# The join of a graph layer and two attentions: row sums added early, graph sums added from PSUM, three projected rows ahead

## The reference, cut to what matters

```python
xn = _layernorm(x)
x2 = x + _L0_gnn_ref(xn, edge_index, ...) + _L0_mix_ref(xn[None], ...)[0]
out = x2 + _L0_ffn_ref(_layernorm(x2)[None], ...)[0]
# _L0_gnn_ref: two relational layers; a layer sums over each node's incoming edges
# _L0_mix_ref: kernel attention of 12 heads; its end, with x meaning xn:
y = xn + heads @ W_proj + b_proj
return (y - mu) * rsqrt(var + LN_EPS) * gamma + beta
# _L0_ffn_ref: softmax attention of 12 heads on the normalised x2, with a router
# (x2n @ Wg.T) and low-rank parts (x2n @ A) that need "logits" of 136 columns per row
```

## Time and profile before

| what | us |
|---|---|
| median of 3 runs (lowest, highest) | 2971.27 (2967.63, 2975.25) |
| the profiled execution, its own time | 2969.1 |
| its span, first to last instruction | 2967.3 |
| mean granted TensorE clock, share of 2.4 GHz | 0.955 |

### The profile page before, as it was taken

One profiled execution on the slowest core, in us unless ns is written; L12 is line 12 of the kernel. 1 busy time (PEld: TensorE's weight loads), 2 busy tenths in 40 slices (PEclk: granted clock), 3 DMA queues, 4 the chain that ended last, 5 costly groups with the idle time before them and its releaser, 6 DMA issues.

```text
span 2967.3 us, 65252 instructions
## 1 busy us (share of the span) xinstructions
PE 2651.6 (89%) x22950; PEld 1938.8 (65%) x22950; DVE 1584.1 (53%) x2845; ACT 777.7 (26%) x1100; POOL 1277.2 (43%) x1363
## 2 busy tenths in 40 slices
PE   5998999978998769999999898876769999999999
PEld 4787888847676557888885667754545556555555
DVE  7566666664545553333334354544775745746731
ACT  2111121201222212111220132211134355354350
POOL 1684211147777710000006677774415274274372
PEclk9999999999999979999999899987979999999999
DMA  5233333459989932333237988997310000000013
GB/s 165 90 127 103 121 123 118 146 197 314 321 298 307 313 126 90 104 121 99 94 99 251 331 291 302 323 339 241 96 38 1 22 22 1 22 22 1 22 48 94
DMA packets 102525, 440.92 MB, mean 149 GB/s; under 512 B 19881, under 2 KB 20204, under 8 KB 98081
## 3 DMA queue, kind: packets, MB, share of 16 engines
q0 software_dynamic: 55712, 266.88, 26.4%
q1 hardware_dynamic: 44001, 131.65, 13.8%
q10 hardware_dynamic: 2592, 39.32, 3.7%
HBM read 357.66 MB, written 80.08 MB: 148 GB/s over the span
## 4 chain that ended last, share of the span: by engine, by line
PE 59%; DVE 16%; issue 7%; POOL 7%; DVEq 4%; DMA 4%; ACT 2%; POOLq 0%; SPq 0%; ACTq 0%
PE PS L1709 26%; PE PS L2057 6%; PE PS L1719 3%; PE PS L1987 3%; PE PS L1808 3%; POOL GATA L685 2%; PE PS L1902 2%; DVE NMC L1630 2%; PE PS L2044 2%; PE PS L1846 2%; POOL ROW L685 2%; PE PS L2045 2%; POOL PL L736 2%; PE PS L1840 2%; PE PS L1860 1%
## 5 line engine op out<-in xcount | busy, mean ns | idle before, releaser
L1709 PE MATMUL PS<-WHL,XT 128*125 (+1 forms) x2880 | 487.2, 329 | 7.1 <-DVE WHL L1092 4.2
L1709 PE MATMUL PS<-WHL,HT 128*125 (+1 forms) x2880 | 477.1, 329 | 12.0 <-DVE HT L1245 9.4
L1709 PEld LDWEIGHTS PS<-WHL,HT 128*125 (+1 forms) x2880 | 395.3, 138 | 90.1 <-DVE HT L1245 10.6
L1709 PEld LDWEIGHTS PS<-WHL,XT 128*125 (+1 forms) x2880 | 390.8, 137 | 82.9 <-issue 4.7
L736 POOL TENSOR_TENSOR PL<-PF 125x500 bf16<-125x500 f32 (+1 forms) x360 | 322.4, 928 | 216.4 <-ACT PF L949 215.5
L685 POOL DMA_INDIRECT GATA<-msg_table,SKEY x324 | 311.1, 960 | 138.2 <-issue 96.1
L1179 DVE SCALAR_TENSOR_TENSOR MSG<-PS,MSG 125x768 f16<-125x768 f32 x160 | 153.0, 956 | 360.8 <-ACT MSG L775 358.9
L775 ACT ACTIVATE MSG<-PS 125x768 f16<-125x768 f32 x160 | 129.6, 810 | 794.7 <-PE PS L1709 794.7
L2057 PE MATMUL PS<-PF,V 125*128 125x500 bf16 (+1 forms) x720 | 244.6, 352 | 16.0 <-POOL PL L736 14.4
L685 POOL DMA_INDIRECT ROW<-msg_table,SKEY x216 | 213.0, 986 | 83.6 <-issue 59.6
L949 ACT ACTIVATE PF<-PS,QK 125x500 f32<-125x500 f32 (+1 forms) x360 | 213.5, 608 | 124.3 <-PE PS L2045 118.1
(11 more groups left out here) (316 smaller groups left out, 4803.4 us busy)
## 6 DMA issues: line engine op xcount, KB each, us to landing
msg_table<-MSG SPq DMA_DIRECT2D x160, 336.0 KB
WST<-in_wg_dram ACTq DMA_DIRECT2D x16, 2304.0 KB, 9.9
WST<-in_wf_dram SPq DMA_DIRECT2D x7, 1536.0 KB, 6.8
KROW<-key_rows POOLq DMA_DIRECT2D x54, 192.0 KB, 3.8
WST<-in_wm_dram SPq DMA_DIRECT2D x6, 1152.0 KB, 5.5
msg_table<-MSG SPq DMA_DIRECT2D x160, 39.0 KB
GATA<-msg_table,SKEY POOLq DMA_INDIRECT x324
ROW<-msg_table,SKEY POOLq DMA_INDIRECT x216
```

The costliest lines, as they stand in the source:

```text
L1709: ins = pe.matmul(PS[0:ROWS, b0 + h, 0:HALF], X[:, xp, k, bass.ts(t, ROWS)], panel_part(slot, wp, k, h), start=k == 0 and xp + wp == 0, st ...
```

## The change: what it does

- **Sums of rows early.** At the start of layer 2 POOL loads `xn` and `x` of each row, adds the projection bias to the one and `beta` to the other (`sum_rows`, `sums_out`) and writes them to `xb_rows` and `xg_rows` in DRAM. `join_row` is gone.
- **Graph sums from PSUM.** PE transposes `ACC` as before; DVE's `graph_row` adds the PSUM result to the `xg` row in SBUF (`JX`). ACT's copy and the way through `gnn_rows` are gone. SP loads `XGE` (xg of rows 0 to 2) in the gather's first part, xg of rows 3 to 9 after the last group.
- **Projections.** `M0` and `M1`, the projections of rows 0 and 1, stand behind groups 78 and 80 of layer 2 on PE, that of row 2 between the graph transposes of rows 4 and 5. DVE takes them in `project_row`: rows 0 and 1 before the ten `graph_row`, row t+1 at the end of row t. In PE's loop, turn t is now: transposes of row t, projection of row t+3, logits of row t-1.
- **The panel `wa`** is scaled and split behind the groups like a head pair: X in slot 58, T and Y in 61, B and Z in 68, H and L in 77.
- **Loads moved.** `HF` (the other pairs' heads, 5 loads of 625 KB) is loaded after `q2` of the last pair (slot 66) and no longer after its `o12` (slot 72), followed by xb of rows 0 and 1. For that `HF` lies where `XT` was, and the join writes a new `XT2`.

```diff
-                    if i + 1 < first + LPAIRS and r in AHEAD:
+                    if r in AHEAD and (i + 1 < first + LPAIRS or (L == 1 and AHEAD[r] not in "HL")):
...
-                slots[min(grp + 1 + c, AG)].append((f"D{c}", first + LPAIRS - 1))
+                slots[grp + 1 + c].append((f"D{c}", first + LPAIRS - 1))
+            if L == 1:
+                slots[grp + 4] += [("H", PAIRS), ("L", PAIRS)]
+                slots[grp + 5].append(("M", 0))
+                slots[grp + 7].append(("M", 1))
...
+        def xb_row(t):
+
+            k = (5, 6, 0, 1, 2, 3, 4, 5, 6, 0)[t]
+            return XBS[:, k, :] if k < 5 else WST[0:ROWS, (k - 1) * D:k * D]
...
+                    for j in range(2):
+                        sp.wait_ge(S[f"pre_out{j}"], 2 * ROW_IN * RT // 2)
+                    for t in range(3):
+                        move_rows(sp, XGE[:, t, :], xg_rows[t * ROWS:(t + 1) * ROWS, :], S["xg_in0"])
...
-            sp.dma_start(WST[:, 0:WM], a["wa"]).then_inc(S["w_in"], 16)
+            sp.dma_start(WST[:, 0:WM], a["wa"]).then_inc(S["mw_in"], 16)
             pair_out(4)
-            sp.wait_ge(S["mix_pe"], mix.made(PAIRS - 1, "o12"))
+            sp.wait_ge(S["mix_pe"], mix.made(PAIRS - 1, "q2"))
...
+
+            def load_xb(t, done):
+
+                move_rows(sp, xb_row(t), xb_rows[t * ROWS:(t + 1) * ROWS, :], S[done])
+
+            for t in range(2):
+                load_xb(t, "xb_in0")
             sp.wait_ge(S["group_read"], 2 * AG)
-            for n_, key in enumerate(("bmp", "gamma", "beta")):
-                sp.dma_start(VEC[:, n_, :], a[key].broadcast_to([ROWS, D])).then_inc(S["vec_in"], 16)
-            for t in range(RT):
-                sp.wait_ge(S["gnn_made"], t + 1)
...
+            for t in range(3, 8):
+                move_rows(sp, JX[:, t, :], xg_rows[t * ROWS:(t + 1) * ROWS, :], S["xg_in1"])
+            sp.wait_ge(S["rows_done"], 2)
+            for t in range(8, RT):
+                move_rows(sp, JX[:, t, :], xg_rows[t * ROWS:(t + 1) * ROWS, :], S["xg_in2"])
+            sp.dma_start(GAM[:], a["gamma"].broadcast_to([ROWS, D])).then_inc(S["gam_in"], 16)
+            for t in range(2, 7):
+                load_xb(t, "xb_in1")
+            sp.wait_ge(S["mw_lo"], PAIRS + 1)
+            sp.dma_start(WST[:, 0:WF], a["wf"][0:128, :]).then_inc(S["w_in"], 16)
+            sp.wait_ge(S["gnn_t"], RT)
...
+                if t < 2:
+                    sp.wait_ge(S["mp_free"], 2 + t + 1)
+                    load_xb(7 + t, "xb_in0")
                 sp.wait_ge(S["x2_made"], t + 1)
                 move_rows(sp, x2_rows[t * ROWS:(t + 1) * ROWS, :], ROW[:, t % 2, :], S[f"x2_out{t % 2}"])
-                if t in (0, 3, 4, 5):
-                    load_join({0: 6, 3: 7, 4: 8, 5: 9}[t])
                 if t == 2:
-                    sp.dma_start(WST[:, 0:WF], a["wf"][0:128, :]).then_inc(S["w_in"], 16)
+                    load_xb(9, "xb_in2")
...
+            def sum_rows(t):
+
...
+                move_rows(g, GATF[:, 2 + 2 * j, :], xn_rows[t * ROWS:(t + 1) * ROWS, :], S[f"pre_in{j}"])
+                move_rows(g, GATF[:, 3 + 2 * j, :], a["x"][t * ROWS:(t + 1) * ROWS, :], S[f"pre_in{j}"])
...
+            def sums_out(t):
+
...
+                for n_ in range(2):
+                    g.tensor_tensor(GATF[:, 2 + 2 * j + n_, :], GATF[:, 2 + 2 * j + n_, :], GATF[:, n_, :], ALU.add)
+                g.drain()
+                move_rows(g, xb_rows[t * ROWS:(t + 1) * ROWS, :], GATF[:, 2 + 2 * j, :], S[f"pre_out{j}"])
+                move_rows(g, xg_rows[t * ROWS:(t + 1) * ROWS, :], GATF[:, 3 + 2 * j, :], S[f"pre_out{j}"])
...
             for L in range(2):
                 if L == 1:
+                    g.wait_ge(S["group_read"], AG)
+                    g.wait_ge(S["xn_stored"], ROW_IN * RT)
+                    g.sem_inc(S["tick"], 1)
+                    for n_, key in enumerate(("bmp", "beta")):
+                        g.dma_start(GATF[:, n_, :], a[key].broadcast_to([ROWS, D])).then_inc(S["vec_in"], 16)
+                    sum_rows(0)
+                    g.wait_ge(S["vec_in"], 32)
+                    for t in range(RT):
+                        if t + 1 < RT:
+                            sum_rows(t + 1)
+                        sums_out(t)
                     for r in range(REL):
...
+                    for j in range(2):
+                        g.wait_ge(S[f"pre_out{j}"], 2 * ROW_IN * RT // 2)
...
-            def join_row(t):
-
-                g.wait_ge(S[f"jr_in{JSLOT[t]}"], 3 * ROW_IN * (2 if t > 5 else 1))
-                rows = join_rows(t)
-                g.tensor_tensor(rows[:, 0, :], rows[:, 0, :], VEC[:, 0, :], ALU.add)
-                g.tensor_tensor(rows[:, 1, :], rows[:, 1, :], rows[:, 2, :], ALU.add)
-                g.drain()
-                g.tensor_tensor(rows[:, 1, :], rows[:, 1, :], VEC[:, 2, :], ALU.add)
-                g.drain()
-                g.sem_inc(S["jr_made"], 1)
-
-            scale(W_LORA)
-            g.wait_ge(S["vec_in"], 3 * 16)
-            for t in range(RT):
-                join_row(t)
...
-                            act.activation(WMX[:, 0, :], WST[:, 0:WM], ACT.Copy, scale=MSC[:, WSCALE]).then_inc(S["mw_hi"], 1)
+                            if i == PAIRS:
+                                act.wait_ge(S["hf_made"], 3 * PAIRS)
+                            act.activation(WMX[:, 0, :] if i < PAIRS else WHM[:, 0, 0, :], WST[:, 0:WM], ACT.Copy, scale=MSC[:, WSCALE]).then_inc(S["mw_hi"], 1)
...
-                        v.scalar_tensor_tensor(WMX[:, 1, :], WST[:, 0:WM], MSC[:, WSCALE], WMX[:, 0, :], ALU.mult, ALU.subtract).then_inc(S["mw_lo"], 1)
+                        high, low = (WMX[:, w, :] if i < PAIRS else WHM[:, 0, w, :] for w in range(2))
+                        v.scalar_tensor_tensor(low, WST[:, 0:WM], MSC[:, WSCALE], high, ALU.mult, ALU.subtract).then_inc(S["mw_lo"], 1)
...
-                v.scalar_tensor_tensor(xtview(XT, 1, t), tview(4 + 2 * (t % 2)), X_SCALE, xtview(XT, 0, t), ALU.mult, ALU.subtract).then_inc(S["xf_free"], 1)
+                v.scalar_tensor_tensor(xtview(XT2, 1, t), tview(2 * (t % 2)), X_SCALE, xtview(XT2, 0, t), ALU.mult, ALU.subtract).then_inc(S["xf_free"], 1)
...
-
-            panel_max(W_LORA, WM)
-            split_low(W_LORA, WHM, WM)
-            v.wait_ge(S["gnn_t"], RT)
...
+            def project_row(t):
+
+                v.wait_ge(S["mp_done"], t + 1)
+                if t in (0, 2, 7, 9):
+                    v.wait_ge(S["xb_in0" if t in (0, 7) else "xb_in1" if t == 2 else "xb_in2"], {0: 2, 2: 5, 7: 4, 9: 1}[t] * ROW_IN)
+                if t >= 2:
+                    v.wait_ge(S[f"x2_out{t % 2}"], ROW_IN * (t // 2))
+                    v.wait_ge(S["xf_made"], t - 1)
+                v.tensor_tensor(halves(ROW[:, t % 2, :]), rowps(4 + 2 * (t % 2)), halves(xb_row(t)), ALU.add).then_inc(S["mp_free"], 1)
+
+            def graph_row(t):
...
+                v.wait_ge(S["gnn_t"], t + 1)
+                if t in (0, 3, 8):
+                    v.wait_ge(S[f"xg_in{(0, 3, 8).index(t)}"], {0: 3, 3: 5, 8: 2}[t] * ROW_IN)
+                v.tensor_tensor(halves(JX[:, t, :]), rowps(2 * (t % 2)), halves(XGE[:, t, :] if t < 3 else JX[:, t, :]), ALU.add).then_inc(S["jx_made"], 1)
+
+            project_row(0)
+            project_row(1)
+            for t in range(RT):
+                graph_row(t)
             v.memset(HG[:], 0.0)
             v.drain()
...
+            v.wait_ge(S["gam_in"], 16)
             for t in range(RT):
...
-                v.wait_ge(S["mp_done"], t + 1)
-                v.wait_ge(S["jr_made"], t + 1)
-                if t >= 2:
-                    v.wait_ge(S[f"x2_out{t % 2}"], ROW_IN * (t // 2))
-                v.tensor_tensor(halves(row), rowps(2 * (t % 2)), halves(join_rows(t)[:, 0, :]), ALU.add).then_inc(S["mp_free"], 1)
-                v.drain()
                 join_statistics(t)
                 if t == 2:
                     v.wait_ge(S["lg_in"], 32)
                 if t >= 2:
                     take_logits(t - 2)
...
-                v.scalar_tensor_tensor(row, row, STAT[:, t % 2, 12:13], VEC[:, 1, :], ALU.subtract, ALU.mult)
-                v.drain()
-                v.scalar_tensor_tensor(row, row, STAT[:, t % 2, 16:17], join_rows(t)[:, 1, :], ALU.mult, ALU.add).then_inc(S["x2_made"], 1)
+                v.scalar_tensor_tensor(row, row, STAT[:, t % 2, 12:13], GAM[:], ALU.subtract, ALU.mult)
+                v.drain()
+                v.scalar_tensor_tensor(row, row, STAT[:, t % 2, 16:17], JX[:, t, :], ALU.mult, ALU.add).then_inc(S["x2_made"], 1)
...
+                if 1 <= t < RT - 1:
+                    project_row(t + 1)
                 if t == 5:
                     panel_max(W_FFN, WF)
...
+                        elif r == "M":
+                            projection(i)
...
-            for t in range(RT):
+
+            def graph_transposes(t):
+
                 if t >= 2:
-                    pe.wait_ge(S["gnn_made"], t - 1)
...
```

(48 more changed lines are left out.)

79 lines of the change are left out of this document (32 added, 47 removed).

## The result

The change makes the kernel slower: 3029.87 us (median of four executions, 3026.75 to 3035.93) against 2969.45 us for the kernel before in the same job (2967.39 to 2975.25). The ratio is 1.0203, with a 95% interval of 1.0179 to 1.0227. The forecast was 3014 and its range 2997 to 3030, so the sign is right, and the time lies 0.13 us inside the range's upper end: +60.4 us where +45 was forecast, and outside the 3005 to 3022 that the forecast case had by its own terms.

A forecast was written before the change was run, and what follows sets the result against it. The prediction saw latency in the join's lead-in and a ring of waits through every loop row. It summed 2969.1 + 40.5 (loop) + 2 (lead-in) + 1.5 (additions) + 1 (traffic) = 3014 us, range 2997 to 3030.

The forecast's parts named there:

- the forecast case: The whole kernel at 3014 us, from 3005 to 3022 by its own terms, chance 0.72.
- The ring: Join loop: row end, ScalarE, transposes, logits, take; projection enters it, 20.4 us a turn instead of 13.5, loop +40.5.
- The rivals with VectorE or a warm TensorE setting the pace: Join loop: VectorE sets the pace, 2947 us, chance 0.05; TensorE stays at its upper level, 3000 us, chance 0.10.
- Moved additions: Start of layer 2: GpSimd's 20 additions are hidden from POOL but meet VectorE, +1.5 us.
- I take one hit: Layer 2: one of 20 GpSimd additions delays VectorE on the path, 1.5 us; all 20 would be 27.
- the bound of 5: Layer 2: the most that TensorE's four waits for VectorE's HT make likely for the additions, 5 us.
- A hit's price: VectorE's operation with two SBUF inputs takes 2.39 us beside GpSimd's additions, 1.02 without: 1.37 us per hit.
- Traffic: Layer 2's gather: five new rows, 1.92 MB, cost 6.0 us if DMA sets the pace, 0 if GpSimd; taken as +1.
- The maximum and its steps: Layer 2's gather: X, T, Y, B, Z lie where GpSimd's issue sets the pace and cost nothing.
- The price named for the uncovered case, 5: Layer 2's gather: X, T, Y, B, Z without cover would cost another 5 us or so.
- The lead-in from the last group: Last group's end to row 0's statistics: 32 us instead of 37.8, but starting 7.7 later, +2 net.
- the rival "the tail is worse": M0 wholly at the lower level (+6.5), traffic in full (+5), most hits (+3.5): 3029 us, chance 0.10.

The follow-up runs named there:

- Two experiments, one on each kernel: Kernel after with logits ahead of the projection: 2979.78 us, ratio 0.9998; kernel before with the projection ahead of logits: 3027.32 us, ratio 1.0157.
- six of its side effects undone or placed better: Kernel after with logits first, GpSimd's sums, maximum and third projection later, HF late, no early xg rows: 2955.60 us, ratio 0.9920 against the kernel before.

## Why the prediction was right in sign and short in size

- **The ring**, +40.5 forecast, +40.0 measured (131.5 to 171.5). Two experiments, one on each kernel, show that the order of projection and logits makes it. The three parts came out too: the first take 30.6 us behind row 0's statistics (30.3 forecast), five turns of 20.2 (20.4), and 39.4 from the take in row 7 to the end (39.4). The rule that matmuls keep the program's order (the Trainium skill, "TensorE: Matmul & The Clock Gate", section "Step-by-step: what each phase is for") agrees with all four orders seen here. The rivals with VectorE or a warm TensorE setting the pace fall: VectorE waits in every row, and the transposes stayed at 1.51 us behind 8.35 us of idling.
- **Moved additions**, +1.5 forecast. This is a failed step: "I take one hit". In the first trace five splits were hit, for 13.2 us of VectorE's time (3.52 + 4.07 + 2.57 and two smaller), of which 3.8 reached TensorE; over all traces it is 6.6, so even the bound of 5 was too low. A hit's price was wrong too: 1.37 holds for the loop of before, where no operation of 1.02 us took more than 2.41, but a split that met a pair waited for all of it in nearly every case. The rule that I weighed, that the loser waits for the whole of the other instruction (the Trainium skill, "SBUF — State Buffer", section "SBUF: two separate sides"), comes nearer, but one addition of 1.8 us isn't the bound either: the traces show waits over two, of 3.52 and 4.07 us in the first.
- **Traffic**, +1 forecast, "as issues follow each other without a gap". This is the other failed step. The window that I read the earlier trace rows had both GpSimd and the DMA engines near their limit, and I sided with GpSimd. Where the loads really fell, groups 13 to 15 and 69 to 71, the DMA share was 1.01 and 1.02, and in the first of them 1.00 before the change. The `xg` rows cost 4.8 us, more than the 3.6 that their 1.15 MB take at the 318 GB/s of the earlier trace rows, and "the same bytes" of `HF` cost 4.6 us or more by their earlier place alone.
- **The maximum and its steps**, forecast at nothing, "where GpSimd's issue sets the pace". They lay in groups 60 and 61, where TensorE waited for VectorE's indicators (3.9 us, 1.3 before): +3.8 in the first trace, 3.2 on the means of all (12.45 against 9.27). The price named for the uncovered case, 5, was the better guess.
- **M0**, 7.7 us late forecast, 4.9 measured. It took 9.0 us (forecast 9.5), but the indicators of both groups behind it were ready, not of one alone; group 80 followed in 2.3 us.
- **The lead-in from the last group**, 32 forecast, 28.9 measured, although VectorE waited for the third projection, 7.44 us, which the forecast had in line on TensorE alone. TensorE's own line, M1, ten rows of transposes and the third projection, took 25.1 us where 28.4 was forecast. Loads cost nothing there, until that wait was gone.

So the sum was short by 12.6 us against the profile before: additions 2.3, traffic 10.5 (5.2 + 6.3 - 1; the experiments trace 3.4 to 4.8 of the 5.2 and 4.6 of the 6.3 to the loads), maximum 3.8 and the unassigned rest some 2, less 2.8 for M0 and 3.2 for the lead-in. That the time still fell inside the range is luck: 18.6 us of misses were offset by 6.0 the other way, and 0.13 us were to spare. It is luck as well that the rival "the tail is worse" gave 3029: its M0 wholly at the lower level (+6.5) did not occur, and traffic and the maximum, which it had at +5 and nothing, cost more than it allowed.

The change's idea itself is sound on this evidence: the join without the trip shortens the lead-in by 8.9 us, and with six of its side effects undone or placed better the kernel is 0.8% faster than before.

## What to carry to other kernels

Work made ahead of need must also be issued behind what is needed now: on an engine that keeps its order, a projection three rows early, placed in front of logits due at once, doubled the length of a turn, and swapping two statements took it back. Before costing moved work at nothing, look at the very groups into which it falls, for each engine and for the DMA share, and not at a mean window nearby: the same 2.55 us cost 4 us in one place and nothing in the groups to which they were moved. When an edit looks free, ask what hides it; the late rows of `xg` cost nothing until the projection that hid them was moved.

## What the runs showed of the hardware beyond the forecast

- Two additions of GpSimd in a line held VectorE for both: splits of 0.94 us took 4.46 and 5.01. An operation with one tensor input in SBUF (L1256, 0.60 us) was held as well, for 3.18.
- In the loop of before GpSimd's additions follow one another as well, yet VectorE's operations of 1.02 us took 2.41 at most, and additions of 1.80 up to 2.53. Why splits lose a whole pair and these operations don't is open.
- It goes the other way too: beside VectorE's split with two inputs (2.62 us) an issue of a gather on GpSimd took 2.83 us instead of 0.95. In the gather of layer 2 in the kernels before and after, each of the six issues of more than 2 us (2.36 to 2.98) lies beside such a split and ends 0.8 us behind it.
- TensorE's idle time between turns cost twice in the ring: the 8.35 us itself, and work at a lower granted clock behind it (0.50 during the transposes, the lower of the two levels; 1.00 in the turn without such idle time). The projection's first twenty matmuls took 8.39 us behind cold transposes and 6.66 behind warm ones, the same matmuls 1.7 us apart.
- The gather of layer 1, unchanged code, took between 406.3 and 417.6 us from trace to trace, so a single total could not have settled any of the edits of 4 to 8 us; the stage tables did.
